# A two-layer transformer kernel on one core: semaphores that count from zero, and one block per stage

## The reference

```
x = x + windowed_attention(layernorm(x), Wq, Wk, Wv, Wp)     # 16 heads, window of 128 to each side
x = x + moe(layernorm(x), gate_w, w_up, w_down, shared)      # 8 experts, top 2 of them, plus a shared one
x = x + block_attention(layernorm(x), Wq, Wk, Wv)            # blocks of 64, first and last attend to all
x = x + ternary_linear(layernorm(x), weight, alpha, bias)    # weights quantized to -1, 0, 1
```

## Time and profile before

| | |
|---|---|
| median of 3 runs | 2747.41 us (2745.48 to 2752.2) |
| the profiled execution | 2753.61 us |
| its span, first to last instruction | 2751.9 us |
| TensorE matmul busy | 2235.0 us (81%) |
| VectorE busy | 1884.6 us (68%) |
| ScalarE busy | 1690.2 us (61%) |
| GpSimd busy | 1072.2 us (39%) |

### The profile page before, as it was taken

One profiled execution on the slowest core, in us unless ns is written; L12 is line 12 of the kernel. 1 busy time (PEld: TensorE's weight loads), 2 busy tenths in 40 slices (PEclk: granted clock), 3 DMA queues, 4 the chain that ended last, 5 costly groups with the idle time before them and its releaser, 6 DMA issues. The chain is left out here.

```text
span 2751.9 us, 72387 instructions
## 1 busy us (share of the span) xinstructions
PE 2235.0 (81%) x25421; PEld 1285.4 (47%) x25421; DVE 1884.6 (68%) x5615; ACT 1690.2 (61%) x3876; POOL 1072.2 (39%) x1325
## 2 busy tenths in 40 slices
PE   6946888888876488869999994982999999998365
PEld 4622333333324376758888882550343433333143
DVE  4537888888835567754444445755999999995365
ACT  6934777777761255524444444770888888889142
POOL 3522444444447578746666662440000000000154
PEclk9976999999988799989999997995999999999587
DMA  6542222222203166755553434863122222221187
GB/s 215 184 149 50 78 79 76 75 76 78 79 22 116 55 168 177 173 143 119 138 136 92 92 83 136 267 211 95 51 69 74 69 75 69 75 70 32 48 163 174
DMA packets 393758, 297.97 MB, mean 108 GB/s; under 512 B 258592, under 2 KB 326944, under 8 KB 393408
## 3 DMA queue, kind: packets, MB, share of 16 engines
q1 hardware_dynamic: 380256, 257.41, 35.2%
q0 software_dynamic: 12960, 35.60, 3.8%
q10 hardware_dynamic: 192, 0.33, 0.0%
HBM read 133.53 MB, written 123.69 MB: 93 GB/s over the span
## 5 line engine op out<-in xcount | busy, mean ns | idle before, releaser
L717 ACT ACTIVATE a_pr<-a_pst 128x384 f32<-128x384 f32 (+3 forms) x2176 | 934.5, 482 | 226.4 <-PE a_pst L752 189.4
L665 DVE TENSOR_REDUCE a_mx<-a_psc 128x1 f32<-128x384 f32 (+2 forms) x1152 | 587.7, 565 | 45.5 <-PE a_psc L752 35.9
L818 PE MATMUL a_po<-a_pr,a_ve 128*17 128x128 f32 (+3 forms) x10496 | 566.6, 304 | 2.2 <-ACT a_pr L717 1.3
L660 DVE CUSTOM_DVE_ANT_0 a_cut<-a_psc,row_mask 128x384 bf16<-128x384 f32 (+1 forms) x1024 | 497.3, 522 | 89.5 <-PE a_psc L752 43.5
L752 PE MATMUL a_psc<-a_ke,a_qe 52*128 52x128 f16 (+5 forms) x3072 | 375.5, 289 | 165.9 <-DVE a_mx L660 52.9
L639 POOL TENSOR_SCALAR_AFFINE_SELECT a_pr<-a_pr 128x512 f32<-128x512 f32 x448 | 275.0, 634 | 373.6 <-ACT a_pr L717 373.6
L752 PE MATMUL a_pst<-a_qe,a_ke 53*128 53x128 f16 (+5 forms) x3072 | 368.2, 284 | 41.7 <-ACT a_pr L717 19.8
L752 PEld LDWEIGHTS a_psc<-a_ke,a_qe 52*128 52x128 f16 (+1 forms) x3072 | 123.2, 94 | 362.2 <-DVE a_mx L660 186.1
L818 PEld LDWEIGHTS a_po<-a_pr,a_ve 128*17 128x17 f32 x10496 | 194.3, 96 | 186.6 <-issue 131.2
L877 POOL MEMSET t_spread<- 128x2048 f32 x1 | 1.8, 1805 | 717.1 <-POOLq L93 717.1
L752 PEld LDWEIGHTS a_pst<-a_qe,a_ke 53*128 53x128 f16 (+1 forms) x3072 | 113.6, 93 | 357.3 <-ACT a_pr L717 324.1
(11 more groups left out here) (233 smaller groups left out, 4257.9 us busy)
## 6 DMA issues: line engine op xcount, KB each, us to landing
a_qe<-qx SPq DMA_DIRECT2D x384, 64.0 KB, 2.8
a_ke<-kx SPq DMA_DIRECT2D x384, 64.0 KB, 2.8
vx<-p_vst SPq DMA_DIRECT2D x32, 544.0 KB, 3.0
a_ve<-vx SPq DMA_DIRECT2D x64, 272.0 KB, 3.2
ox<-a_ost SPq DMA_DIRECT2D x256, 68.0 KB
qx<-p_stg SPq DMA_DIRECT2D x64, 256.0 KB, 2.8
kx<-p_stg SPq DMA_DIRECT2D x64, 256.0 KB, 3.1
x_res<-x SPq DMA_DIRECT2D x16, 512.0 KB, 8.9
```

The lines of the kernel that those rows point to most:

```text
L660: dve.tensor_tensor_reduce(out=cut[:, n % 4, 0:width], in0=psc[(u * n_s + n) % RING][:, 0:width], in1=row_mask[:, at:at + width], scale=1. ...
L665: dve.tensor_reduce(out.unsqueeze(1), psc[(u * n_s + n) % RING][:, 0:width], AXX, ALU.max)\
L717: act.activation(pr[s % SLOTS][:, h // 2, h % 2, 0:width], pst[prob_slot(u, n) % RING][:, 0:width], ACT.Exp, scale=scale).then_inc(p_ready, 1)
L818: last = pe.matmul(po[h][32 * a:32 * a + VW, tok % CH:tok % CH + w], ve[g][:, t, a * VW:(a + 1) * VW], pr[s % SLOTS][:, a // 2, a % 2, col ...
```

## The change

All semaphores count from zero, so `ONE` and the `start()` blocks go. Each stage has semaphores of its own, with numbers that no other stage of the same half uses, so nothing has to be cleared between two stages of a half. The first half is c, p0, a0, c0 and g, the second e, p1, a1 and t. An object `Epoch` gathers the semaphores of a half and clears them in one block at its end: once between g and e, and once after t. The semaphores of the indirect DMAs are now made once in `build` and handed in. A stage's own block holds the same instructions in the same order as before, with `wait_ge(sem, value)` for `wait_ge(sem, ONE + value)`.

```diff
-class Semaphores:
...
-    def start(self):
-        with self.nc.Block() as block:
-            @block.gpsimd
-            def _(pool):
-                for s in self.taken:
-                    pool.sem_inc(s, ONE)
-
-    def clear(self):
-        with self.nc.Block() as block:
-            @block.gpsimd
-            def _(pool):
-                for s in self.taken + self.unset:
-                    pool.sem_clear(s)
...
+class Epoch:
+    def __init__(self, nc, ctx):
+        self.nc, self.ctx, self.taken = nc, ctx, []
         ctx.callback(self.clear)
+    def named(self, tag):
+        def sem(name):
+            return self.also(self.ctx.enter_context(self.nc.semaphore(f"{tag}_{name}")))
+        return sem
+
+    def also(self, s):
+        self.taken.append(s)
+        return s
+
+    def clear(self):
+        with self.nc.Block() as block:
+            @block.gpsimd
+            def _(pool):
+                for s in self.taken:
                     pool.sem_clear(s)
...
-        sem = Semaphores(nc, ctx, tag)
+        sem = epoch.named(tag)
...
-        sem.start()
         block = ctx.enter_context(nc.Block())
...
-                sp.wait_ge(qk_stored[k], ONE + B // 2 * 8 * 16)
+                sp.wait_ge(qk_stored[k], B // 2 * 8 * 16)
...
+        with ExitStack() as first:
+            epoch = Epoch(nc, first)
+            stage_constants(nc, epoch, ident, ident16, row_mask, mrow)
...
+            stage_route(nc, epoch, "g", x_res, mean, rstd, ident, gate_w, up_w, down_w, ew, rt, xs, x2, by_route)
+        with ExitStack() as second:
+            epoch = Epoch(nc, second)
+            stage_routed(nc, epoch, "e", x_res, ident, ew, rt, xs, y2, x2, by_routed)
...
+            stage_close(nc, epoch, "t", x_res, ident, ox, tern_w, tern_alpha, tern_bias, out)
```

More of the change, by code:

```diff
@@ L132, in finish @@
         dve.tensor_tensor(var, st[:, :, 2], st[:, :, 5], ALU.add).then_inc(self.step, 1)
-        dve.wait_ge(self.step, ONE + 3)
+        dve.wait_ge(self.step, 3)
         dve.tensor_scalar(self.mean[:, :], total, 0.5, None, ALU.mult).then_inc(self.step, 1)
@@ L335, in norm @@
                 if c >= 2:
-                    act.wait_ge(turned, ONE + EC * (c - 1))
-                act.wait_ge(shifted, ONE + c + 1)
+                    act.wait_ge(turned, EC * (c - 1))
+                act.wait_ge(shifted, c + 1)
                 for t in range(TC):
@@ L351, in queries_keys @@
                 if b >= 2 and c % 2 == 0:
-                    act.wait_ge(qk_stored[b % 2], ONE + 128 * (b // 2))
+                    act.wait_ge(qk_stored[b % 2], 128 * (b // 2))
                 for m in range(4):
@@ L367, in _ @@
             norm(0)
-            act.wait_ge(s_w, ONE + 64)
+            act.wait_ge(s_w, 64)
             for j in range(3):
@@ L372, in _ @@
             high(0)
-            act.wait_ge(s_bqk, ONE + 1)
+            act.wait_ge(s_bqk, 1)
             for c in range(NC):
@@ L692, in turn @@
                 bank = turned_bank(u - 1)
-                act.wait_ge(m_turned, ONE + u + 1)
-                counted(act, m_loaded[(g + 2) % HG], (b * 64 if g >= 2 else (b - 1) * 64 + 64))
+                act.wait_ge(m_turned, u + 1)
+                after(act, m_loaded[(g + 2) % HG], (b * 64 if g >= 2 else (b - 1) * 64 + 64))
                 act.activation(mt[g % 2][:, :], pst[bank][0:4 * TB, 0:P // 2].bitcast(F16), ACT.Copy)\
@@ L699, in copy_out @@
                 u = unit(g, b)
-                counted(act, o_stored[g % 2], b * 128 + (g // 2) * 64)
-                act.wait_ge(p_used, ONE + u * nj + last_of[h] + 1)
+                after(act, o_stored[g % 2], b * 128 + (g // 2) * 64)
+                act.wait_ge(p_used, u * nj + last_of[h] + 1)
                 act.activation(ost[g % 2][:, h, :], po[h][:, :], ACT.Copy).then_inc(o_copied[h], 1)
@@ L710, in step @@
                     width = sum(p[1] for p in pieces)
-                    counted(act, p_used, u * nj + s - SLOTS + 1)
+                    after(act, p_used, u * nj + s - SLOTS + 1)
                     for h in range(4):
@@ L715, in step @@
                             turn(*after_cur)
-                        act.wait_ge(t_ready, ONE + u * n_s + n + 1)
+                        act.wait_ge(t_ready, u * n_s + n + 1)
                         act.activation(pr[s % SLOTS][:, h // 2, h % 2, 0:width],
@@ L1129, in stage_route @@
         gated, ranked, routed = sem("gated"), sem("ranked"), sem("routed")
-        scattered = [sem.from_zero(f"scattered{r}") for r in range(XR)]
+        scattered = [epoch.also(s) for s in scattered]
         gu_ready = [sem(f"gu_ready{f}") for f in range(FC)]
@@ L1242, in row_hi @@
                 if c:
-                    act.wait_ge(row_low, ONE + c)
+                    act.wait_ge(row_low, c)
                 for t in range(TC):
@@ L1260, in silu @@
                 u = 2 * s + h
-                act.wait_ge(gu_ready[f], ONE + u + 1)
+                act.wait_ge(gu_ready[f], u + 1)
                 act.activation(gate[:, f, :], pgu[f][:, 0, :], ACT.Silu, scale=PS).then_inc(gate_done[f], 1)
@@ L1437, in _ @@
                 weight_lo(n)
[L1438 to L1439 removed]
+            dve.wait_ge(made, 12)
+            dve.wait_ge(cleared, 1)
             top2(0)
@@ L1558, in stage_routed @@
         y_ready, y_copied = sem("y_ready"), sem("y_copied")
-        scattered = [sem.from_zero(f"scattered{g}") for g in range(GR)]
+        scattered = [epoch.also(s) for s in scattered]
         x_loaded = sem("x_loaded")
         AD = 8
-        sem.start()
         block = ctx.enter_context(nc.Block())
```

456 lines of the change are left out of this document (219 added, 237 removed).

## The result

The changed kernel takes 2725.45 us (2725.11 to 2731.3, 4 runs) against 2746.44 us (2745.43 to 2752.2, 4 runs). The ratio is 0.9924 with an interval from 0.9905 to 0.9944: 21.0 us less, or 15 to 26.

What follows compares the result with a forecast made beforehand. Stages bound most of the span; between them only helper blocks do, 42.7 of 2751.9 us. Removing increments (21.0 us) and barriers (4.0) takes the median 2747.4 to 2722.4 us; likeliest 2722, range 2714 to 2731.

Steps and rivals of the forecast that it cites:

- The stretches as the whole effect: Between stages no engine does work that counts; helper blocks hold SyncE 42.7 us, and time removed there comes off the total.
- The increments, 21.0 us: At the stage starts, all 250 increments go: 19.8 us at 0.079 each, plus 1.2 us for four hiccups.
- The clears only move: All 257 clears stay, saving nothing: 139 between g and e (9.8 us), 118 at the end (8.3 us).
- rival of slow clears: In the two long clear series, a hiccup of 0.3 us once in thirty loses 2.6 us; above 4 us, 5 in 100.
- The barriers, 4.0 us: Eighteen helper blocks become two, so 16 barriers go at 0.25 us each; bounds 3.2 and 4.8 us.
- The sum: Over the whole kernel, 21.0 for increments plus 4.0 for barriers saves 25.0 us, between 24.2 and 25.8.
- TensorE's clock: At every stage boundary the clock still falls to 1.2 GHz, as TensorE's pauses stay above 14.3 us; no time taken for it.
- The rival of a slow start: Stage e's matmuls stay slow after TensorE's longer pause, 0.022 us more each; 2788 us at 3,000 matmuls; 2 in 100.
- Code loads: At seven boundaries without blocks, engines wait for code: 1.0 us each gives 2729 (5 in 100), 2.8 each 2742 (4 in 100).

Runs made afterwards that it cites:

- the pauses put back: Gathered kernel with range clears, plus two blocks ahead of each stage repeating the old clears and increments on one spare semaphore: 2746.92 us against 2747.99 for the kernel before.
- gathered kernels with range clears: The changed kernel with one clearing instruction per run of adjacent semaphore numbers, run twice: 2706.24 us against 2746.87 and 2707.57 against 2749.50 for the kernel before.
- the first experiment: Kernel before without increments and their nine blocks; each stage still clears its own semaphores in its own block: 2725.06 us against 2746.87.
- the second experiment: Kernel before with its increments kept, but the clears gathered into two blocks of 139 and 118: 2744.34 us against 2746.87.
- the one that clears three times: The changed kernel with each semaphore cleared three times over, 514 clears more in the same two blocks: 2761.58 us against 2749.50 for the kernel before.

## Why the prediction was right

**The stretches as the whole effect.** The prediction read the helper blocks as time in which nothing else goes on, so that every microsecond taken out of them comes off the total. This is shown to within some 4 us: with the pauses put back the time of before came back, and the two gathered kernels with range clears, which wait 40.7 us less than the kernel before, took 40.6 and 41.9 us less. Over all comparisons the measured change lies within 3.6 us of the accounted one.

**The increments, 21.0 us.** The first experiment took them and their nine blocks out, for which the prediction's terms give 21.0 + 9 x 0.25 = 23.2 us; its measured 21.8 has an interval of 18 to 25. In the trace SyncE's 22.4 us of waits in these blocks are gone, 23.0 with its way into them.

**The clears only move.** Also right, with one small mis-sizing: 139 and 118 clears took 10.1 and 8.6 us where 9.8 and 8.3 were forecast, since each series has one hiccup now. That is 0.6 us of the sum. One of 0.4 us stood in a clearing block of the kernel before too, behind its 30 clears between a0 and c0, which the prediction didn't count. Its rival of slow clears, a hiccup once in thirty and 2.6 us of loss, is answered by this: it is two in 257.

**The barriers, 4.0 us.** Seven of them and little else went in the second experiment, for 2.5 us with an interval from 1 to 6, which bears 0.25 each out only roughly. The traces do it better: in the first experiment SyncE's 20.1 us of waits and its way into nine blocks make 20.7; less 257 x 0.071 = 18.2 for the clears and 0.3 for one hiccup, 2.2 us are left, 0.24 for each block. An empty block takes 0.33, outside of the prediction's 0.2 to 0.3; that term was sized for blocks that have something in them and holds for these.

**The sum.** 25.0 us forecast, 24.6 in the trace, 21.0 and 26.1 in the two timed comparisons. 2722 us was forecast; the medians were 2725.45 and 2721.94. How close a single median comes is luck: two of the same kernel lie 3.5 us apart.

**TensorE's clock.** It was at 1.2 GHz in the boundary stretches, as forecast. The reason that the prediction gave, that TensorE's pauses stay long enough, is not what decides it ahead of stage e. With range clears the clock fell some 9 us before the wait there began, while TensorE was running out of work at the end of stage g, so the pause between the stages had no part in that fall. (The 31.7 us ahead of p1 weren't the longest pause either; t's was 33.4.) The wait at e came to 19.3 us in one profile and 18.6 in the other, 18 to 19 having been forecast, and that at a0 to 19.9, for some 20. Stage e came up no slower: in its first 19.9 us it got through 122 and 124 matmuls in two profiles of before, 115 and 130 in two of the changed kernel, 127 and 122 behind the pauses of 13.0 and 30.7 us, and then 182 in 19.6 us before and after. The 115 come from its first load, which landed some 0.7 us later in that profile. The rival of a slow start is refuted by these.

**Code loads.** This rival is refuted too. The first load of a0 is issued 0.1 us behind the barrier without the cover of two blocks, and so is SyncE's first instruction in all the other stages. The prediction had also priced the rival by the wrong packets. It took the 215 of queue q8, 16 KB and 1.0 us each. The page has a second instruction queue; these are its rows in the kernel before, the changed kernel and the one that clears three times:

```profile
q14 instruction: 135, 1.11, 0.1%
q14 instruction: 133, 1.09, 0.1%
q14 instruction: 137, 1.12, 0.1%
```

The 514 further instructions on GpSimd bring four more packets of 8 KB in q14, one for some 128, while q8 has 215 in every profile. So GpSimd's code comes through q14. At 128 instructions each its 133 packets are also about the 17,000 instructions that the trace of the changed kernel has on the four engines other than TensorE, so SyncE's code belongs to them as well. A packet takes some 0.4 us there, and seven in the open would have cost 3 us and not 7. The Trainium skill's statement that a sequencer fetches ahead (Runtime: NRT & Kernel Launch, "Instruction fetch mechanics") agrees with the starts of the stages; its exception for taken branches did not come into play at the ends of these blocks. Fetching is not wholly hidden, though: see the hiccups below.

## What to carry to other kernels

Look for stretches of a trace in which no engine and no queue does anything: their instructions don't count as busy, so they appear only as waits, of SyncE's queue above all, and what was taken out of them here came off the total, to within some 4 us of 25 to 42. Semaphore housekeeping was paid by the instruction (0.07 to 0.08 us) and by the block (0.25 us beyond its instructions, 0.33 to 0.38 empty), so first use an instruction that does many at once, and only then ask where to put it. When a measured gain differs from the accounted one by a few tenths of a per cent, profile both kernels again before giving the difference a cause.

## What the runs showed of the hardware

- A clear of one semaphore has a duration of 44 ns in the profile but comes every 0.071 us; an increment 17 ns and every 0.079. A clear of a range takes longer with its length: 0.77 us for the long one in the middle and 0.65 for that at the end, which together with the two short ones clear 257 semaphores, about 6 ns for each.
- Series of such instructions have hiccups of 0.3 to 0.4 us. All 30 of them in the thirteen profiles stand at the same place of a 128 in GpSimd's list of instructions. Two neighbours in the kernel that clears three times, with 128 clears from each hiccup to the next:

```profile
L95 POOLq EVENT_SEMAPHORE_RANGE_CLEAR  x128: 44/44/44, 1202.2 to 1211.2; - x128
L95 POOLq EVENT_SEMAPHORE_RANGE_CLEAR  x128: 44/44/44, 1211.5 to 1220.5; - x128
```

  Behind each hiccup, by 0.7 to 1.0 us, a packet of 8 KB of code starts in queue q14, and there is one such packet for 128 instructions. That ties the hiccups to the fetching of code; what the sequencer waits for in them is not shown.
- The matmul stages differ by up to 8 us in 2700 between executions of one kernel. In both profiles of the changed kernel stage c0 began at a lower granted clock for longer than in the second profile of before. These are the stretches of 11 us from shortly before its first matmul, changed kernel first:

```profile
827.00:838.00 11.00, 8.55 (x11) 3.33 (x12) 4.62 (x7) 3.15 (x5) 5.96 (x6) 0.66 0.52 195
```
```profile
842.00:853.00 11.00, 9.10 (x32) 4.77 (x33) 5.10 (x8) 4.41 (x7) 6.91 (x7) 0.85 0.52 197
```

  11 matmuls against 32 in the same time. From release to release the stage took 103.2 us in both profiles of the changed kernel, and 101.4 and 100.9 in those of before. The first profile of the gathered kernel with range clears, whose pause ahead of c0 is the same, did not show it, so it is left open whether it belongs to that kernel or to when it ran.
